# TensorE's program for the 32 experts: a hardware loop over four-expert bodies, or all of it written out

## The reference, cut to what matters

```
x = x + gnn(layernorm(x))                      # 64 blocks of 128 rows, width 384
# ffn(layernorm(x)): rows are gathered into 8 x 16 slots per block, these into 8 x 4 x 4 second slots
u   = einsum('bGkemd,kedh->bGkemh', slots2, w1) + b1     # k = 8, e = 4: 32 experts, 384 -> 2 x 1024
v, gate = split(u, 2, axis=-1)
act = v * gelu(gate)
o   = einsum('bGkemh,kehd->bGkemd', act, w2) + b2        # 1024 -> 384
# o goes back to the slots and from there to the rows
x = x + ffn(...)
```

## Time and profile before

| | |
|---|---|
| median of three runs | 3081.5 us (3080.99 to 3088.55) |
| profiled execution, its span | 3075.87 us, 3074.1 us |
| TensorE busy (matmul), of the span | 2860.1 us, 93% |
| VectorE, ScalarE, GpSimd busy | 62%, 49%, 48% |
| mean granted TensorE clock | 0.975 |
| instruction fetches: queue q8, queue q14 | 95 packets with 1.56 MB, 34 packets with 0.28 MB |

### The profile page before, as it was taken

How to read it: one execution, slowest core, us unless ns; L and a number is a source line. 1 busy time by engine, 2 the same in 40 slices (tenths; PEclk the granted TensorE clock), 3 DMA queues, 4 the chain that set the end, 5 groups by cost and what they waited for, 6 DMA issues and landing times. The chain is left out here.

```text
span 3074.1 us, 63137 instructions
## 1 busy us (share of the span) xinstructions
PE 2860.1 (93%) x21971; PEld 2754.7 (90%) x21971; DVE 1899.1 (62%) x3029; ACT 1510.8 (49%) x3986; POOL 1474.9 (48%) x1486
## 2 busy tenths in 40 slices
PE   2899999999999999999999848997999999999996
PEld 2899999999999999999999738997999999999993
DVE  3466666666666666666666425664776766676764
ACT  3355554545454555545554425675454444454540
POOL 0344444343534444443444324552776766676760
PEclk9899999999999999999999969998999999999999
DMA  3010101010100101010101034553666656665899
GB/s 130 13 42 26 46 26 46 26 46 25 42 28 31 41 26 46 26 46 26 46 26 41 20 94 119 150 148 119 200 209 199 209 182 198 193 208 173 252 322 340
DMA packets 276793, 321.59 MB, mean 105 GB/s; under 512 B 17304, under 2 KB 275608, under 8 KB 276504
## 3 DMA queue, kind: packets, MB, share of 16 engines
q1 hardware_dynamic: 267960, 307.17, 32.1%
q10 hardware_dynamic: 8704, 12.58, 1.1%
HBM read 260.97 MB, written 58.72 MB: 104 GB/s over the span
## 5 line engine op out<-in xcount | busy, mean ns | idle before, releaser
L1567 PE MATMUL u_bank<-x_in,x_w 128*128 128x256 f32 x4608 | 584.1, 286 | 28.5 <-issue 20.8
L1567 PEld LDWEIGHTS u_bank<-x_in,x_w 128*128 128x128 f32 x4608 | 576.9, 194 | 31.4 <-issue 31.4
L949 POOL TENSOR_TENSOR hT_lo<-h_tmp,hT_hi 128x512 fp32r<-128x512 f32 x192 | 246.6, 1285 | 454.3 <-DVE hT_hi L838 453.1
L1724 POOL TENSOR_TENSOR x_aT<-x_act,x_aT 128x512 fp32r<-128x512 f32 x128 | 299.3, 2339 | 216.7 <-ACT x_aT L1632 216.7
L411 PE MATMUL m_bank<-yT_hi,w_hi 128*128 128x256 f32 x1152 | 341.5, 296 | 1.5 <-ACT h_tmp L683 1.5
L1623 ACT ACTIVATE x_gelu<-u_bank,x_b1T 128x256 f32<-128x256 f32 x256 | 121.4, 474 | 444.9 <-PE u_bank L1567 444.9
L411 PE MATMUL m_bank<-yT_hi,w_lo 128*128 128x256 f32 x1152 | 323.4, 281 | 0.0
L411 PE MATMUL m_bank<-yT_lo,w_hi 128*128 128x256 f32 x1152 | 323.4, 281 | 0.0
L1720 POOL TENSOR_TENSOR x_w<-expert_raw,x_w 128x768 fp32r<-128x768 f32 x128 | 274.3, 2143 | 102.1 <-DVE x_w L1663 102.1
L683 ACT ACTIVATE h_tmp<-m_bank,b1c 128x256 f32<-128x256 f32 x384 | 156.9, 470 | 273.5 <-PE m_bank L411 273.1
L1579 PE MATMUL o_bank<-x_w,x_aT 128*128 128x384 f32 x1536 | 289.3, 336 | 1.8 <-POOL x_aT L1724 1.8
(11 more groups left out here) (216 smaller groups left out, 6939.2 us busy)
## 6 DMA issues: line engine op xcount, KB each, us to landing
expert_raw<-in_L_ffn_w_dram SPq DMA_DIRECT2D x384, 384.0 KB, 5.0
ws_raw<-in_L_ffn_w_slot_dram SPq DMA_DIRECT2D x32, 576.0 KB, 7.1
x_in<-in_x_dram SPq DMA_DIRECT2D x32, 384.0 KB, 3.4
x_res<-in_x_dram SPq DMA_DIRECT2D x32, 384.0 KB
residual<-f_sb SPq DMA_DIRECT2D x32, 384.0 KB, 2.5
yn<-yn_sb SPq DMA_DIRECT2D x32, 384.0 KB, 2.5
expert_out<-x_o SPq DMA_DIRECT2D x64, 192.0 KB, 3.2
slots2T<-residual SPq DMA_DIRECT2D x8, 1536.0 KB, 11.7
```

What stands on the lines that cost most here:

```text
L949: nc.gpsimd.tensor_tensor(hT[i % 3][1][:], h_tmp[i % 2][:], hT[i % 3][0][:].bitcast(F32), ALU.subtract).then_inc(hl.sem, 1)
L1567: mm = pe.matmul(u_bank[n % BANKS][:, g, :], w1s[i % 2][a][:, c, g, c2 * P:(c2 + 1) * P], xT[e % 2][b][:, c, :], start=c == 0 and j == 0, ...
L1724: nc.gpsimd.tensor_tensor(aTs[i % 2][1][:], aT[i % 2][:], aTs[i % 2][0][:].bitcast(F32), ALU.subtract).then_inc(al.sem, 1)
```

## The change

TensorE no longer goes through `over_experts`. Its 32 experts are written out one after the other, with Python integers for x. The buffer parities are the same as before, since `1 - e` with e = x % 2 names the other of two buffers, as `(e - 1) % E2` did after its use `% 2`. The order of the matmuls, their operands and the semaphores are unchanged. ScalarE, VectorE, GpSimd and SyncE keep `over_experts` and its loop.

```diff
-            def body(x, k, e):
+            def body(x, e):
                 up(x, e, 0)
                 if past(x, 1):
-                    down(x - 1, (e - 1) % E2, PIECES - 1)
+                    down(x - 1, 1 - e, PIECES - 1)
                 for i in range(1, PIECES):
                     up(x, e, i)
                     down(x, e, i - 1)
-            over_experts(pe, body)
-            down(NX - 1, E2 - 1, PIECES - 1)
+            for x in range(NX):
+                body(x, x % 2)
+            down(NX - 1, 1, PIECES - 1)
```

## The result

The changed kernel takes 3045.0 us, the median of four runs (3041.63 to 3046.94), against 3081.24 us before (3076.13 to 3088.55). The ratio is 0.9879, with a 95% interval from 0.9858 to 0.9901. Forecast were 3046 us in a range of 3034 to 3060. The profiled execution took 3045.31 us, of which its instructions span 3043.5.

What follows compares the result with a forecast made beforehand. TensorE, busy 93% of the span, was taken as the bound; removing 22.9 us of pauses and 11.4 us of low clock (34.3 us) gave 3041.6 to 3047.2 us, taken as 3046, range 3034 to 3060.

Steps and rivals of the forecast that it cites:

- the stage's windows: Experts' stage cut into seven stretches of four experts: five, at 105.88 to 112.15 us, would fall to 102.29, saving 34.3.
- pauses: Ten TensorE stalls in the experts' stage, two behind each of five branches back, 22.9 us in all, would go.
- low clock: TensorE matmuls at granted clock 0.50 behind four of five branches back; full speed would return the other 11.4 us.
- Which base: Whole kernel: gain taken from the profiled execution gives 3041.6 us, from the median, 5.6 us higher, 3047.2; 3046 was taken.
- the one wait on VectorE's split: TensorE's 2.1 us wait at expert 20, named for VectorE's split of w1, was counted as instruction issue, not data.
- The register instructions: Instructions computing wait values in registers in TensorE's expert loop; removing them was costed at nothing.
- The crossings of blocks: TensorE's straight expert code passing from one 16 KB code block to the next; costed at nothing.
- rival C: Slower: crossings between blocks of TensorE's straight expert code pause some 2.2 us each, 37 of them, 3128 us; chance 0.04.
- The other engines' branches: Four other engines still branch back in the experts' stage, 0.04 to 0.07 us each, hidden within 1.3 us of cover.
- rival A: GpSimd or weight DMA comes late after each of the other engines' branches, 2 us at five places: 3057 us; chance 0.07.

Runs made afterwards that it cites:

- the loop of two experts: Changed kernel, but TensorE walks experts 4 to 27 in a hardware loop with two experts per trip (12 trips): 3044.38 us, ratio 0.9884.
- the loop of eight: Changed kernel, but TensorE walks experts 4 to 27 in a hardware loop with eight experts per trip (3 trips), branch not announced: 3058.03 us, ratio 0.9932.
- the loop at slot 232: Kernel before, with TensorE's four-expert loop kept and its first instruction placed 232 instructions into a 16 KB code block: 3087.31 us, ratio 1.0014.

## Why the prediction was right

- **The bound.** TensorE alone set the pace of the stage, and a pause taken from it was a gain in full. Shown: the stage's windows went to 102.3 us and the whole followed.
- **The sum.** The terms were 34.3 us for the windows, of which 22.9 us were pauses and 11.4 us low clock. The same seven stretches give it back exactly, each at 102.29 or 102.30 us. Expert 0 gave 1.0 us more (27.15 us before, 26.14 after), but that is a matter of the execution: it took 25.70 to 27.08 us in the ten others. Of the 11.4 us I was too quick to call all of it low clock. The four stretches at 0.50 hold 20.1 busy us, which at full speed are 10.1 us less; the other 1.4 us are not the clock's. In the window of the first branch TensorE is busy for 0.53 us more than in a window without a branch although its clock stayed at 1.00. The sum does not change. The measured medians are 36 us apart. The surplus of less than 2 us is within the spread of the medians.
- **Which base.** I took 3046, between 3041.6 and 3047.2. The runs lie from 3041.6 to 3046.9 and their median at 3045.0. That it came within 1 us is luck, since no row said where in these 5.6 us the answer lay, and the repeat of the same kernel has its median at 3043.14. Part of why one execution lies above another is that the experts begin up to 8 us later or earlier. In the profiled pair 3.2 of the 4.4 us arose in the first 190 us; what causes it stays open.
- **The second reading of the waits.** I put the one wait on VectorE's split down to issue. It is gone with the branch, and it came back, once among ten pauses, when only the placement was made worse. It was a name for the same pause.
- **Costed at nothing.** The register instructions: the loop of two experts has them in twelve trips and is as fast. The crossings of blocks: none showed in 24 experts, nor in 97 blocks of the graph layer (rival C refuted). The other engines' branches: written out or not, no difference (rival A refuted).
- **What was imprecise.** I wrote that the body of 98 KB was code that is no longer at hand, as if by its size. The runs show that it can be kept: with its head at the start of a block it is, and 232 instructions further on it is not. The cause was a placement that made it one block too many, not the loop and not the size. This did not change the forecast, but it changes the remedy: one argument of the loop gives all that writing out 20 more experts gives.
- **The size of one branch** is not fixed: 3.6 to 9.9 us before, 7.2 and 7.3 in the loop of eight, 43 us over five in the loop at slot 232. The pauses set it, and the clock behind them adds to it. The split between the two was read from the trace and not tested on its own, since I had no kernel with the same pauses and a clock that stays.

## What to carry to other kernels

Where one engine is the bound and has a hardware loop, look at its compare-and-branch on the loop's own line: some 0.2 us is a branch into code at hand, and several us are a refetch. The fetch queue's blocks per trip tell the same (none, or all of them). The pause may stand as two, one at the target and one a few matmuls later, and may be named a wait for data. Before writing the loop out, place its head, make the body smaller or announce the branch: each of the three was as fast here. The last was so only because the body could then be kept, as the loop of eight shows, and by the count of blocks the first needs such a body too.

## What the runs showed of the hardware that I had not expected

- TensorE keeps eight blocks of 16 KB. This is inferred from counts of fetched blocks and two placements, not seen as such: a body that touched seven was kept, together with the block past its end, one that touched eight was kept when its branch was announced and nothing past its end was fetched, and one placed to touch eight without the announcement was fetched anew with nine blocks per trip, although only one was too many.
- An announced branch kept the body from being fetched at all (0 blocks over five trips against 44), so it changes which block is fetched ahead, and not only when. The fetch that is gone is the one past the loop's end: the seventh of the first trip, 1.3 us ahead of the branch, is absent, and the loop of eight fetches 14 blocks per trip in the place of 15.
- A taken branch into code at hand takes TensorE's sequencer 215 ns, against 45 to 56 ns in the compare-and-branch of the others, and is hidden behind the queued matmuls all the same.
- Where the body is too long to be kept, the announcement brings the target's block and not the one behind it: 2.07 and 1.57 us were left.
